# A normalised recurrence beside a small FFN: chunks moved from the free axis to the partitions, one step and one transpose at a time

## The reference, cut to what matters

```python
q = einsum('btc,dc->btd', xn, Wq);  v = einsum('btc,dc->btd', xn, Wv)
O_lh = polar_orthogonal(W_lh);  O_rh = polar_orthogonal(W_rh)   # 12 iterations X <- 1.5 X - 0.5 X X^T X
def step(h, q_t):                                            # 512 steps, one after another
    h_new = rms(h @ O_lh.T + q_t @ O_rh.T)                   # rms(z) = z / sqrt(mean(z*z) + 1e-6)
    return h_new, h_new
attn = einsum('btc,dc->btd', qs * v, Wc)                     # qs: all h_new
real = xn @ cos(theta + theta_noise);  imag = xn @ sin(phi + phi_noise)
ffn = sqrt(real*real + imag*imag)
out = x + attn + ffn
```

## Time and profile before

| | |
|---|---|
| median of 3 runs | 170.09 us (169.5 to 170.56) |
| span of the profiled execution | 168.3 us |
| what lies around the span, by the median | 1.8 us |
| TensorE matmul busy | 149.2 us (89%) |
| VectorE busy | 130.5 us (78%) |
| ScalarE busy | 116.7 us (69%) |
| GpSimd busy | 103.3 us (61%) |
| mean granted TensorE clock | 0.973 of full |

### The profile page before, as it was taken

One profiled execution on the slowest core, in us unless ns is written; L12 is line 12 of the kernel. 1 busy time (PEld: TensorE's weight loads), 2 busy tenths in 40 slices (PEclk: granted clock), 3 DMA queues, 4 the chain that ended last, 5 costly groups with the idle time before them and its releaser, 6 DMA issues.

```text
span 168.3 us, 3931 instructions
## 1 busy us (share of the span) xinstructions
PE 149.2 (89%) x1068; PEld 126.7 (75%) x1068; DVE 130.5 (78%) x549; ACT 116.7 (69%) x482; POOL 103.3 (61%) x241
## 2 busy tenths in 40 slices
PE   6888888789999999999879999999599999999900
PEld 6866777478888888987667777777498888889800
DVE  6599998498888999998987777777946666666860
ACT  3147999957766889999767777777557677676600
POOL 7007777123443477899837777777659787877700
PEclk9999999999999999999999999999969999999985
DMA  4880000000000000000000000000000003030330
GB/s 100 240 300 1 4 2 0 0 4 2 0 0 6 0 0 4 4 0 0 2 6 0 0 0 0 6 2 0 0 0 6 0 0 127 6 125 0 125 125 10
DMA packets 3497, 5.06 MB, mean 30 GB/s; under 512 B 464, under 2 KB 1616, under 8 KB 3472
## 3 DMA queue, kind: packets, MB, share of 16 engines
q1 hardware_dynamic: 3168, 4.46, 8.5%
q0 software_dynamic: 160, 0.26, 0.5%
q10 hardware_dynamic: 144, 0.07, 0.1%
HBM read 2.69 MB, written 2.10 MB: 28 GB/s over the span
## 4 chain that ended last, share of the span: by engine, by line
PE 56%; DVE 31%; issue 7%; ACT 3%; DVEq 0%
PE bank L869 16%; PE bank L856 14%; DVE MIX L698 9%; PE bank L867 6%; PE bank L835 4%; DVE FS L664 4%; DVE WT L705 4%; PE bank L821 3%; PE bank L776 3%; PE bank L762 2%; DVE EDGE_RI L607 2%; DVE PXT L566 2%; PE bank L753 2%; PE bank L727 2%; ACT RT L447 2%
## 5 line engine op out<-in xcount | busy, mean ns | idle before, releaser
L350 POOL TENSOR_TENSOR Q<-RT 128x128 bf16<-128x128 f32 (+1 forms) x108 | 50.8, 471 | 40.5 <-ACT RT L447 39.5
L698 DVE TENSOR_TENSOR MIX<-UT,RT 128x128 f32<-128x128 f32 x108 | 39.2, 363 | 19.3 <-ACT RT L447 15.4
L856 PE MATMUL bank<-WT,PXT 128*128 128x128 f32 x212 | 48.4, 310 | 4.1 <-DVE WT L694 3.5
L447 ACT ACTIVATE RT<-bank 128x128 f32<-128x128 f32 x108 | 29.9, 277 | 23.9 <-PE bank L869 23.0
L869 PE MATMUL bank<-SQ,MEAN 128*128 128x128 f32 (+1 forms) x180 | 41.9, 292 | 0.4
L856 PEld LDWEIGHTS bank<-WT,PXT 128*128 128x128 f32 x212 | 32.1, 191 | 10.0 <-DVE WT L694 4.3
L441 ACT ACTIVATE SQ<-WT 128x128 f32<-128x128 f32 (+1 forms) x106 | 32.5, 307 | 6.3 <-DVE WT L694 2.9
L869 PEld LDWEIGHTS bank<-SQ,MEAN 128*128 128x128 f32 (+1 forms) x180 | 24.6, 165 | 11.1 <-ACT SQ L441 9.2
L705 DVE TENSOR_TENSOR WT<-MIX,bank 128x128 f32<-128x128 f32 x102 | 28.4, 278 | 4.6 <-DVE MIX L698 0.5
L867 PE MATMUL bank<-Q,EPS_MEAN 128*128 128x128 bf16 (+1 forms) x140 | 29.4, 245 | 0.0
L821 PE MATMUL bank<-CS,XNT 128*128 128x128 f32 x128 | 25.4, 280 | 0.0
(11 more groups left out here) (132 smaller groups left out, 235.4 us busy)
## 6 DMA issues: line engine op xcount, KB each, us to landing
X<-in_L_attn_x_dram SPq DMA_DIRECT2D x8, 256.0 KB, 6.1
out_dram<-OUT SPq DMA_DIRECT2D x6, 256.0 KB, 2.8
out_dram<-OUT SPq DMA_DIRECT2D x4, 128.0 KB, 2.1
WP<-in_L_attn_W_rh_dram ACTq DMA_DIRECT2D x1, 64.0 KB, 2.0
WP<-in_L_attn_W_lh_dram SPq DMA_DIRECT2D x1, 64.0 KB, 2.2
ANG<-in_L_ffn_theta_dram POOLq DMA_DIRECT2D x1, 64.0 KB, 4.2
WV<-in_L_attn_Wv_dram SPq DMA_DIRECT2D x1, 64.0 KB, 4.0
ANG<-in_L_ffn_phi_dram POOLq DMA_DIRECT2D x1, 64.0 KB, 4.0
```

The lines of the kernel that those rows point to most:

```text
L350: pool.tensor_tensor(split((Q16 if guess(at) else Q)[g][:, :]), r, r, ALU.mult).then_inc(q_ready[g], 1)
L447: act.activation(r_of(j, g), split(SUM[g][:, 0:P]), ACT.Sqrt).then_inc(r_ready[g], 1)
L698: dve.tensor_tensor(split(MIX[g][:, :]), split(UT[:, cols(j, g)]), r_before(j, g), ALU.mult).then_inc(m_ready[g], 1)
L856: pe.matmul(split(Y[g][:, 0:P]), OT[0][:, :], w, start=True, stop=True).then_inc(y_ready[g], 1)
```

## The change

Chunks go to the partitions and channels to the free axis. The state `W[g]` is `[chunk, channel]` with one more column, which always holds sqrt(1e-6 * 128), the eps column of `UZ` times `r`, plus a zero column of `Y`. So the sum of squares over 129 columns, by ScalarE's accumulating output, already has the eps in it, and `r` is one number a partition (`RT`, one column for a step and group). A step is then one VectorE instruction, `W = UZ*r + Y`. But TensorE needs the state with channels on the partitions, so each step's state is transposed: TensorE transposes (L761) into `TY[g]`, VectorE copies to `WT[g][s%2]` (L587), TensorE multiplies `Y[g] = WT^T OT[0]` (L812). The slot's parts:

```diff
-                        pe.matmul(split(Y[g][:, 0:P]), OT[0][:, :], w, start=True,
-                                  stop=True).then_inc(y_ready[g], 1)
-                        pe.matmul(SUM[g][:, 0:P], eps_mean[:, :], q, start=True, stop=False)
-                        pe.wait_ge(sq_ready[g], done(p, j) + 1)
-                        pe.matmul(SUM[g][:, 0:P], mean[:, :], sq[:, :], start=False,
-                                  stop=True).then_inc(s_ready[g], 1)
+            for n in range(SLOTS + 2):
+                m, g = divmod(n, GROUPS)
+                prev, po = divmod(n - 1, GROUPS)
+                if n < SLOTS:
+                    pe.wait_ge(wt_ready[g], m + 1)
+                    pe.matmul(Y[g][:, 0:P], stationary(m, g), OT[0][:, :], start=True, stop=True).then_inc(y1_done[g], 1)
+                if 0 < n <= SLOTS:
+                    transposed(prev + 1, po)
+                if n < len(LATE):
+                    pair(NEARLY + n)
+                for h in FFN_SLOTS.get(n, ()):
+                    ffn(h)
+                if n in V_SLOTS:
+                    values(V_SLOTS[n])
+                if 0 <= n - 2 - OUT0 < TILES:
+                    projected(n - 2 - OUT0)
```

ScalarE, where `norm_of_state` replaces L441 and L447:

```diff
+            def norm_of_state(s, g):
...
+                act.activation(SQE[:, 0:E], state(s, g)[:, 0:E], ACT.Square,
+                               accum_out=SSE[:, g:g + 1]).then_inc(ss_ready[g], 1)
+                act.wait_ge(ss_ready[g], s + 1)
+                t = tile(state_step(s), g)
+                act.activation(RT[:, t:t + 1], SSE[:, g:g + 1], ACT.Sqrt, scale=1.0 / C).then_inc(r_ready[g], 1)
```

VectorE:

```diff
-                        dve.wait_ge(r_ready[g], i)
-                        dve.tensor_tensor(split(MIX[g][:, :]), split(UT[:, cols(j, g)]), r_before(j, g),
-                                          ALU.mult).then_inc(m_ready[g], 1)
-                        side_work(side_slot(at, n), again)
-                        dve.tensor_tensor(state(j, g), split(MIX[g][:, :]), split(Y[g][:, 0:P]),
-                                          ALU.add).then_inc(w_ready[g], 1)
+            def one_step(n, m, g, j):
...
+                dve.wait_ge(r_ready[g], m + 1)
+                dve.wait_ge(y1_done[g], m + 1)
+                dve.scalar_tensor_tensor(out=W[g][:, 0:E], in0=UZ[:, uz(j, g), 0:E], scalar=norm_of(m, g),
+                                         in1=Y[g][:, 0:E], op0=ALU.mult, op1=ALU.add).then_inc(w_ready[g], 1)
+                prev, po = divmod(n - 1, GROUPS)
+                if ends_pass(prev + 1):
+                    end_scaled(prev + 1, po)
+                transposed(prev + 1, po)
```

More of the change, by code:

```diff
@@ L747, in transpose_tiles @@
                     pe.wait_ge(S["xt_copied"], b - 1)
-                for k in range(half * BT // 2, (half + 1) * BT // 2):
+                for k in range(BT):
                     j, g = divmod(b * BT + k, GROUPS)
@@ new lines, in _ @@
+            pe.wait_ge(pxt_copied[1], POLAR_ITERS + 1)
+            pe.matmul(GRAM[0][:, 0:P], WQ[:, :], OT[1][:, :], start=True, stop=True).then_inc(S["mt_done"], 1)
+            pe.wait_ge(pxt_copied[0], POLAR_ITERS + 1)
+            pe.wait_ge(S["mt_copied"], 1)
+            for g in range(GROUPS):
+                last = pe.matmul(FB[0][:, g * P:(g + 1) * P], XNT[:, cols(FIRST, g)], MT[:, :], start=True, stop=True)
+            last.then_inc(S["u_first"], 1)
+            for b in range(POLAR_ITERS - LN_ITER - 4, BATCHES):
+                transpose_tiles(b)
@@ new lines, in transposed @@
+            def transposed(s, g):
+                if s == 0:
+                    pe.wait_ge(S["u_first_copied"], 1)
+                else:
+                    pe.wait_ge(w_ready[g], s)
+                if ends_pass(s):
+                    pe.wait_ge(diag_ready[g], bounds_before(s) + 1)
+                    pe.matmul(TY[g][:, 0:P], W[g][:, 0:P], DIAG[g][:, :], start=True,
+                              stop=True).then_inc(t_done[g], 1)
+                else:
+                    pe.transpose(TY[g][:, 0:P], state(s, g)[:, 0:P], IDENT[:, :]).then_inc(t_done[g], 1)
@@ new lines, in pair, with ffn @@
+            def pair(i):
+                q, g = PAIRS[i]
+                if i < 2:
+                    pe.wait_ge(S["xt_copied"], BATCHES - 1 + i)
+                else:
+                    pe.wait_ge(S["uz_copied"], i - 1)
+                b = PJ[i % 2]
+                for k in range(pair_width(q)):
+                    last = pe.matmul(b[:, k * P:(k + 1) * P], XNT[:, cols(2 * q + k, g)], MT[:, :], start=True, stop=True)
+                last.then_inc(S["uz_done"], 1)
+            def ffn(h):
+                f, i = divmod(h, 2)
+                if h == 0:
+                    pe.wait_ge(S["cs_done"], 1)
+                if i == 0 and f >= 2:
+                    pe.wait_ge(S["ffn_sq"], f - 1)
+                pe.matmul(FB[f % 2][:, i * 2 * P:(i + 1) * 2 * P], XNT[:, h * P:(h + 1) * P], CS[:, :],
+                          start=True, stop=True).then_inc(S["ffn_done"], 1)
@@ new lines, in values @@
+            def values(i):
+                b, half = divmod(i, 2)
+                if i == 0:
+                    pe.wait_ge(S["uz_copied"], len(PAIRS))
+                if half == 0 and b >= 2:
+                    pe.wait_ge(S["v_copied"], b - 1)
+                pe.matmul(PJ[b % 2][:, half * 2 * P:(half + 1) * 2 * P], WVT[:, :],
+                          XNT[:, b * BANK + half * 2 * P:b * BANK + (half + 1) * 2 * P],
+                          start=True, stop=True).then_inc(S["v_done"], 1)
```

750 lines of the change are left out of this document (338 added, 412 removed).

## The result

| | before | changed |
|---|---|---|
| median (runs) | 170.32 us (4; 169.5 to 170.58) | 221.95 us (4; 221.44 to 222.11) |
| span of the profiled execution | 168.3 us | 218.6 us (its time: 222.01) |
| mean granted TensorE clock | 0.973 | 0.719 |

The ratio is 1.3047, 95% interval 1.3009 to 1.3084: slower by 51.6 us. The forecast of 192.5 (179 to 203) had the direction and missed 29.4 us of the size.

What follows compares the result with a forecast made beforehand. The prediction took the bound to be an ordered recurrence loop, not one engine's load. Start 36.8, slots 129.4, pass ends 5.7, side matmuls 2.0, tail 10.8, clock 6 and 1.8 around the span gave 192.5 us (179 to 203).

Steps and rivals of the forecast that it cites:

- Which loop closes: Claim that step, copy, matmul Y and next step form the loop across both groups, 1.125 us a slot.
- The way back: Last piece of each slot, from the end of matmul Y to the next step's start on VectorE: 0.03 us.
- The clock: TensorE's clock was expected to fall in slots 42 to 83, adding 6 us; pass 3 charged nothing.
- Ends of passes: Reciprocal, scaled identity and matmul delay the copy by 0.95 us at two groups' three pass ends: 5.7 us.
- Wide side matmuls: FFN and v matmuls of 256 columns on TensorE overrun some slots, 2.0 us in all.
- Start: Time before the first step, put at 36.8 us where it was 35.70.
- Tail and what lies around: Time behind the last step, 10.8 us, plus the 1.8 by which the median exceeds the profiled span.
- The clock holds: Rival: TensorE's clock does not fall, so its 6 us drop out and the time is 186.5 us; chance 0.23.
- ScalarE as the bound: Rival: ScalarE sets slots 12 to 41 if the accumulating square costs 0.2 us more; about 198 us, chance 0.15.
- Each group's own loop: Rival: the copy does not wait for the other group's step, 0.84 us a slot, 158 us; chance 0.05.
- break-even: Slot length at which the changed kernel would match the old one's span, put at 0.98 us.

Runs made afterwards that it cites:

- e4_swap: Changed kernel with VectorE's copy of slot n-1's transposed state placed ahead of the step of slot n: 193.78 us.
- e3_waits: Changed kernel with the step waiting for its matmul alone, its other waits taken earlier, ahead of the copy before it: 206.16 us.
- e10_two_waits: Changed kernel with only the eps and u waits moved ahead of the copy, so the step waits for its root and its matmul: 220.95 us.
- e12_all: e11_swap_ends without the added matmuls in slots 84 to 115, and with the step's other waits moved ahead of the copy: 181.08 us.
- e5_waits_warm: Changed kernel with the edits of both e3_waits and e2_warm_all: 193.5 us.
- e2_warm_all: Changed kernel with two extra matmuls of ones in every slot from 43 to the last, pass 3 included: 202.74 us.
- e8_swap_spread: e4_swap with an FFN tile in every second slot and a v tile in every fourth, to slot 74, nothing added: 179.71 us.
- e1_warm2: Changed kernel with two extra matmuls of ones in every slot from 43 to 83, none in pass 3: 211.41 us.
- e11_swap_ends: e8_swap_spread plus matmuls of ones: two in slots 76 to 83, one in 84 to 115, four at each pass end: 173.58 us.

## Why the prediction was wrong, step by step

- **Which loop closes: right.** L619 waits for L812 and L812 for L587, in every pass, and e4_swap broke that loop by one exchange on VectorE. Step to copy, copy, way to TensorE and matmul were each met to 0.01 us.
- **The way back, 0.03 us: mis-sized, and the first of the two steps that failed.** It measured 0.13, so 115 x 0.105 = 12.1 us. The 0.03 came from the earlier trace rows, where L447 stands behind L869. That instruction waits for one semaphore. The step has four waits ahead of it in the code, three of them long satisfied; they were read as free. e3_waits gave the 0.03 back, e10_two_waits puts 0.07 on the second, and e12_all reproduces it on another instruction. (The 12.1 is the term's share of the sum at a slot of 1.23; taking it away at a full clock gave 9.2, e5_waits_warm against e2_warm_all.) The Trainium skill says that an instruction waiting on several engines may have extra instructions with the further waits inserted ahead of it (*Perfetto Trace Analysis*, section *Identifying Dependency Chains*). The queue's piece at L618 agrees in kind, and the runs give the price, which the page does not have; the satisfied second semaphore of e8_swap_spread's copy, which cost nothing, shows that the number of semaphores alone does not set it.
- **The clock, 6 us: the second step that failed, and the larger.** From 98.34 us on there are 65 ordinary distances and 4 ends; at the full clock they would take 65 x 1.23 + 4 x 2.35 = 89.4 us and took 110.8. With the dip at 65 to 68 us (3.78 + 1.46 against 2.77 + 1.23 in e2_warm_all, where the clock held there) that is 22.7 us, 17 more than taken. Three things were off. The price of a slot was read from a matmul of 0.68 that stands where the clock was falling (0.97 granted in the stretch up to 122 us, 0.50 behind it); at the lower level it is 0.80, and the slot 0.31 longer, not 0.19. The 42 slots were multiplied as if the clock came and went; it stayed down. And pass 3 was charged nothing because it has five records a slot: all its slots were at the lower level. e1_warm2 and e2_warm_all, 10.6 and 19.3 us, show both halves.
- **A page against the trace.** By the Trainium skill (*TensorE: Matmul & The Clock Gate*, section *HAM oscillation — how this bites in real kernels*) the clock would have held, since no wait of TensorE in pass 2 has the length that it speaks of. The clock fell; the forecast was right to side with the earlier trace rows and too mild. The next section of that page, *A second HAM failure mode: psum-queue depth-cycling*, ties a coming and going of the clock to short and frequent idle times. That is nearer to pass 2 here, only that it did not come back.
- **Ends of passes, 5.7: a little low.** (2.35 - 1.23) x 6 = 6.7 at the full clock; the scaled identity (L594) takes 0.29, not the 0.17 of a small instruction. **Wide side matmuls, 2.0:** 0.8, of which 0.39 in slot 13 and 0.42 at the second end of pass 0 (2.77 for 2.35). That is the longer slot's doing: at 1.13 us, in e5_waits_warm, they cost about 3. **Start, 36.8:** 37.34. **Tail and what lies around, 12.6:** 222.01 - 209.18 = 12.8, by luck: in the span it is 9.4 instead of 10.8, around it 3.4 instead of 1.8. The 29.4 us are 12.1 (way back) + 17 (clock) + 0.5 (start), with the rest cancelling to some tenths.
- **Rivals.** The clock holds (0.23): refuted. The forecast gave this rival that no wait of TensorE would be above 1 us; at the ends of passes the waits were 1.03 to 1.23. ScalarE as the bound (0.15): refuted, though its suspected price was right to 0.01 (187 ns for reading the accumulator); the slots had the room. Each group's own loop (0.05): not as it stands, but e4_swap comes to 0.98, exactly the slot that the forecast had worked out as break-even. e11_swap_ends, with that slot nearly throughout, is still 3.3 us above the kernel before (1.7%, a small difference): its ends cost 2.38 - 0.98 = 1.40 us each beyond a slot, 8.4 together instead of the 5.7 in that sum. Had the clock been charged for 42 + 31 slots at 0.3 us, the forecast would have been near 208.

Why is it slower than before at all? Of the 51.6 us, 1.6 are the later start (37.34 against 35.70) and none lies behind the last step (12.8 us in both, from the last step to the median). Before, the steps took 157.49 - 35.70 = 121.8 us with their ends of passes and kept TensorE 89% busy. At the full clock the changed ones take 115 x 1.23 = 141.5, 19.7 more, as step, copy and `Y` stand in series, and 11.5 of that are the semaphores (115 x 0.10); the six ends add 6.7, and the clock that an emptier TensorE loses 23.

## What to carry to other kernels

Find the instruction that closes the loop and let it wait for nothing but its last releaser: semaphores known to be up are waited for earlier, on an instruction that is waiting for its own engine anyway, as the copy did in e3_waits. Moved onto the instruction that closes the loop they cost 7.5 us (e12_all). In a serial loop the order of two instructions on one engine (copy, then step) can be worth a fifth of the loop: 0.25 us of a slot of 1.23 here. And a change that empties TensorE has to be charged with the clock, for all the rest of the kernel and at the price of a matmul well inside a slow stretch; spreading work that exists anyway over the slots gave 9.7 of some 23 us back.

## What the hardware showed that was not expected

- The lower clock lasted some 120 us to the kernel's end, 45 us of them with TensorE recorded 4.6 to 4.8 of 5 us busy. With slots of 1.46 and 1.39 instead of 1.51 in pass 3 (e3_waits, e4_swap) it did come back, at about 165 and 157 us. At the lower level the recorded busy share does not tell which will happen: it stayed down at 4.8 of 5 us, and came back behind 4.62 (e4_swap) and 4.92 (e3_waits).
- The same instructions let the clock fall at an end of a pass in one run and not in another (e1_warm2 and e2_warm_all).
- An addition of work made the changed kernel 19 us faster (e2_warm_all).
- A semaphore that is already up and is waited for ahead of the pending one costs about 0.07 us on a VectorE instruction, and one or two more cost 0.03 together. Waited for behind the pending one it cost nothing (e8_swap_spread, pass 3: 0.04 behind the transpose, as with one).
- A square with an accumulated sum is 312 ns and a further 187 ns instruction on ScalarE.
